# Second cross-attention: the score maxima subtracted as three bf16 pieces in one bf16 product

## The reference, cut to what matters

```
q, k, v = query @ wq + bq, key @ wk + bk, value @ wv + bv      # key = value = context, 77 tokens
score = einsum('bhqd,bhkd->bhqk', q, k) / sqrt(16)
score = score + (1 - mask) * -1e9
alpha = softmax(score, axis=-1)                                # subtracts the row's maximum
x = einsum('bhqk,bhkd->bhqd', alpha, v) @ wo + bo
```

## Time and profile before

| | us |
|---|---|
| median of 3 runs (lowest, highest) | 2876.49 (2875.19, 2884.41) |
| the profiled execution, its own time | 2881.71 |
| its span, first to last instruction | 2880.0 |
| outside the span | 1.7 |
| PE busy in the span | 2053.4 |
| DVE busy | 2194.8 |
| ACT busy | 1748.7 |
| mean granted TensorE clock | 0.753 |

### The profile page before, as it was taken

One profiled execution on the slowest core, in us unless ns is written; L12 is line 12 of the kernel. 1 busy time (PEld: TensorE's weight loads), 2 busy tenths in 40 slices (PEclk: granted clock), 3 DMA queues, 4 the chain that ended last, 5 costly groups with the idle time before them and its releaser, 6 DMA issues. The chain is left out here.

```text
span 2880.0 us, 41500 instructions
## 1 busy us (share of the span) xinstructions
PE 2053.4 (71%) x11052; PEld 1159.4 (40%) x11052; DVE 2194.8 (76%) x10063; ACT 1748.7 (61%) x5698; POOL 652.8 (23%) x343
## 2 busy tenths in 40 slices
PE   6232555646556465555657599999999999799997
PEld 3122434434334343343444333334343343465554
DVE  5999999999999999999997355555555555276677
ACT  3678888888888888888881244444444444222221
POOL 0000000000000000000000166766767667200000
PEclk9555556555565555655555699999999999799999
DMA  5742222222222222222210000000000000201100
GB/s 113 152 103 49 50 69 52 55 56 66 49 52 59 63 55 49 58 64 52 55 33 4 4 13 12 13 16 16 11 13 16 15 13 12 88 8 45 41 11 8
DMA packets 86798, 123.55 MB, mean 43 GB/s; under 512 B 17444, under 2 KB 65224, under 8 KB 86600
## 3 DMA queue, kind: packets, MB, share of 16 engines
q1 hardware_dynamic: 86600, 121.37, 17.7%
HBM read 100.33 MB, written 21.00 MB: 42 GB/s over the span
## 5 line engine op out<-in xcount | busy, mean ns | idle before, releaser
L1494 ACT ACTIVATE mix_cand<-mix_pre,mixer_cbuf 128x32 f32<-128x32 f32 x2048 | 591.3, 289 | 166.0 <-DVE mix_pre L1424 82.3
L1491 ACT ACTIVATE mix_cand<-mix_state,mixer_cbuf 128x32 f32<-128x32 f32 x2048 | 652.9, 319 | 34.9 <-DVE mix_state L1416 4.5
L1411 DVE SCALAR_TENSOR_TENSOR mix_prod<-mixer_keys,mixer_cbuf,mix_cand 128x65 f32<-128x65 f32 x2048 | 581.7, 284 | 34.3 <-ACT mix_cand L1494 27.2
L1925 DVE TENSOR_REDUCE self_tops<-self_rough 128x2 f32<-128x1024 f32 x256 | 313.5, 1225 | 365.8 <-PE self_rough L1697 362.6
L1424 DVE SCALAR_TENSOR_TENSOR mix_pre<-mixer_keys,mix_gap,mix_state 128x32 f32<-128x32 f32 x2048 | 526.1, 257 | 27.8
L1523 PE MATMUL mix_out<-all_ident,mix_state 128*128 128x128 f32 x512 | 161.9, 416 | 488.6 <-ACT mix_flat L1475 432.5
L1416 DVE SCALAR_TENSOR_TENSOR mix_state<-mix_cand,mixer_cbuf 128x32 f32<-128x32 f32 x2048 | 507.6, 248 | 0.1
L1911 POOL TENSOR_TENSOR self_psum<-self_psum,self_prob 128x1024 f32<-128x1024 f32 x192 | 451.5, 2352 | 128.3 <-ACT self_prob L1838 118.7
L1838 ACT ACTIVATE self_prob<-self_sco 128x1024 f32<-128x1024 f32 x256 | 260.4, 1024 | 117.1 <-PE self_sco L1710 102.4
L875 POOL TENSOR_TENSOR mix_st_norm_rstd<-mix_st_norm_var,mix_half 128x2 f32<-128x2 f32 x24 | 16.7, 697 | 1316.4 <-DVE mix_st_norm_var L868 1316.4
L1523 PEld LDWEIGHTS mix_out<-all_ident,mix_state 128*128 128x128 f32 x512 | 82.4, 206 | 571.2 <-ACT mix_flat L1475 504.8
(11 more groups left out here) (386 smaller groups left out, 3273.7 us busy)
## 6 DMA issues: line engine op xcount, KB each, us to landing
mixer_keys<-k_rows SPq DMA_DIRECT2D x256, 260.0 KB, 4.9
aT_rows<-self_aT SPq DMA_DIRECT2D x32, 256.0 KB, 2.3
two_aT<-aT_rows SPq DMA_DIRECT2D x8, 1024.0 KB, 7.3
coef_rows<-mixer_coef SPq DMA_DIRECT2D x4, 1280.0 KB, 7.3
mixer_cbuf<-coef_rows SPq DMA_DIRECT2D x64, 80.0 KB, 5.5
k_rows<-mixer_krow SPq DMA_DIRECT2D x32, 65.0 KB, 5.0
proj_xin<-in_xT SPq DMA_DIRECT2D x8, 256.0 KB, 3.3
mix_st_xin<-in_x SPq DMA_DIRECT2D x8, 256.0 KB, 5.5
```

What stands on the lines that cost most here:

```text
L1411: dve.scalar_tensor_tensor(prod[:, b, :], keys[:, h, b, s_, :], coef(NIB, h, s_, b), cand[:, b, s % 2, :], ALU.mult, ALU.mult, accum_out=g ...
L1491: act.activation(cand[:, b, (s + 1) % 2, NS:2 * NS], state[:, hp, sp_, b, :], ACT.Copy, scale=cbuf[:, h, KEEP, b, s_:s_ + 1]).then_inc(kep ...
L1494: act.activation(cand[:, b, (s + 1) % 2, 0:NS], pre[b], ACT.Tanh, scale=cbuf[:, h, BETA, b, s_:s_ + 1]).then_inc(c_ready[b], 1)
L1925: dve.tensor_reduce(tops[:, kh, t, :], rough[:, :, :], AX.X, ALU.max).then_inc(rough_taken, 1)
```

## The change

The maximum of each head is laid as three bf16 numbers whose sum is the f32 value: the first is the value rounded to bf16, the second the rest rounded, the third what is left. `pieces` holds them, `top_dve` makes them by five linked instructions (copy, subtract, copy, subtract, copy), and the two copies into `wide_top` carry 48 columns instead of 16: row 4i + n of a block of 32 holds piece i of head n. `topT` and `minus` become bf16, so the L739 product is a bf16 one over the same 32 rows. `minus` has -1 in the three rows of its head; its pattern comes from one more reduction in the setup (`nths`). The first layer keeps its f32 form.

```diff
-        self.minus = sb("minus", [P, 2 * KT, S2])
+        self.minus = sb("minus", [P, 2 * KT, S2], BF16 if keep_masked else F32)
+        self.ranks = 3 * 2 * KT if keep_masked else 2 * KT
...
-        yield dve.tensor_reduce(self.nth[:, :], self.ident[:, :].rearrange("p (c r) -> p r c", c=QUADS)[:, 0:2 * KT, :], AX.X, ALU.add)
+        yield dve.tensor_reduce(self.nth[:, :], self.ident[:, :].rearrange("p (c r) -> p r c", c=QUADS)[:, 0:self.ranks, :], AX.X, ALU.add)
+        if self.keep_masked:
+
+            yield dve.tensor_reduce(self.nths[:, :], self.nth[:, :].rearrange("p (i n) -> p n i", i=3), AX.X, ALU.add)
...
-        yield dve.tensor_scalar(self.minus[:, :, :], bcast(self.nth[:, :], 2, S2), -1.0, None, ALU.mult)
+        yield dve.tensor_scalar(self.minus[:, :, :], bcast(self.nths[:, :], 2, S2), -1.0, None, ALU.mult)
...
-        ... self.topT = ..., sb("topT", [P, GT])
+        ... self.topT = ..., sb("topT", [P, GT], BF16)
+        self.pieces = sb("pieces", [P, CTILES, 3, H], BF16)
...
-    LINKS = 1 + 1
+    LINKS = 1 + 5 + 1
...
         alone(link(ins))
+
+        for i in range(3):
+            alone(link(dve.tensor_copy(self.pieces[:, :, i, :], self.top[:, :, :])))
+            if i < 2:
+                alone(link(dve.tensor_tensor(self.top[:, :, :], self.top[:, :, :], self.pieces[:, :, i, :], ALU.subtract)))
         for j in range(CTILES):
-            ins = dve.tensor_copy(self.wide_top[:, j, :].rearrange("p (c r) -> p c r", c=QUADS)[:, :, 0:2 * KT].rearrange("p c (f e) -> p f c e", f=KT),
-                                  self.top[:, j, :].rearrange("p (f c e) -> p f c e", f=KT, c=QUADS))
+            ins = dve.tensor_copy(self.wide_top[:, j, :].rearrange("p (c r) -> p c r", c=QUADS)[:, :, 0:3 * 2 * KT].rearrange("p c (n e) -> p n c e", e=2),
+                                  self.pieces[:, j, :, :].rearrange("p i h -> p (i h)").rearrange("p (n c e) -> p n c e", c=QUADS, e=2))
```

More of the change, by code:

```diff
@@ L561, in setup_room @@
         self.piece = sb("piece", [P, B, S2], BF16)
-        self.nth, self.odd = sb("nth", [P, 2 * KT]), sb("odd", [P, 2])
+        self.nth, self.odd = sb("nth", [P, self.ranks]), sb("odd", [P, 2])
+        self.nths = sb("nths", [P, 2 * KT]) if self.keep_masked else self.nth
         self.loaded, self.kv_made, self.k_ready, self.set = sem("loaded"), sem("kv_made"), sem("k_ready"), sem("set")
@@ L641, in setups @@
     def setups(self):
-        return 2 + (not self.keep_masked) + 2 + 3 + 3 * 3 + KT * (1 + 3 * B)
+        return 2 + (not self.keep_masked) + 2 + 3 + self.keep_masked + 3 * 3 + KT * (1 + 3 * B)
 class CrossAttention:
@@ L653, in __init__ @@
         self.q, self.qb, self.prob = sb("q", [P, KT, GT]), sb("qb", [P, KT, GT], BF16), sb("prob", [S2, KT, QUADS, 2, GT])
-        self.top, self.wide_top, self.topT = sb("top", [P, CTILES, H]), sb("wide_top", [P, CTILES, P]), sb("topT", [P, GT])
+        self.top, self.wide_top, self.topT = sb("top", [P, CTILES, H]), sb("wide_top", [P, CTILES, P]), sb("topT", [P, GT], BF16)
+        self.pieces = sb("pieces", [P, CTILES, 3, H], BF16)
         self.rden, self.aT = sb("rden", [P, KT, GT]), sb("aT", [P, KT, GT])
```

## The result

The changed kernel takes 2889.2 us (median of 17 runs) against 2877.3 for the kernel before (17 runs). The ratio is 1.0035, 95% interval 1.0025 to 1.0045: slower by 7 to 13 us, some 10; the two medians lie 11.9 us apart. The profiled execution has a span of 2888.7 us against 2880.0, 8.7 more.

A forecast was written before the change was run, and what follows sets the result against it. PE was taken to bound e0 and the rough half, DVE both wide_top handovers, ACT the exponentials. Group shifts summed to +4.5 or +7.7 us; the middle, +6 on 2876.5, gave 2882.5 us, range 2875 to 2891.

The forecast's parts named there:

- The forecast's own band of +4 to +8: Whole kernel: the likeliest case, +4 to +8 us, 2880 to 2885 us, chance 0.60.
- the late clock: Values: rival that the clock returns late into them, 1.8 us a group over +7.7, +15, 2891 us; chance 0.20.
- The matmuls removed: L739 on PE: bf16 set of four 0.21 us at half clock, saving 0.64 or 0.32 a set, some 15 us PE time.
- The rival that the four do not run abreast: L739 on PE: bf16 products save nothing, DVE steps still paid, some +10, 2886 us; chance 0.04.
- The DVE steps: Handovers through wide_top: five linked instructions and wider copies add 1.2 us each (1.0 to 1.4), uncovered.
- The rival of cheap steps: Handovers through wide_top: added DVE work costs 0.7 us each, total +1.0, 2877.5 us; chance 0.09.
- Group by group: Start of the values, groups 0 to 3: shifts sum to +4.5 us with clock back before f1, +7.7 at the values.
- half-clock branch: f1 scores at 1.2 GHz until the values start: 0, +1.9, +2.9, +2.9 us for groups 0 to 3, sum +7.7.
- so I take the middle, +6: Clock's return around the f1 scores: +6 us chosen between +4.5 (back before f1) and +7.7 (back as values start).
- The prediction's own sign of being wrong: Attention pieces: wrong if the stretch at 0.50 differs by several microseconds, or two f0, not DVE, still releases ACT.
- The setup: Setup of minus: one more reduction (0.2 us) hides in DVE's 1.56 us idle gap, costs nothing; end unchanged.

The follow-up runs named there:

- The runs with 0 to 10 steps: Changed kernel with 0, 3, 5 (as changed) or 10 DVE steps in each handover; ratios to the kernel before 0.9976, 0.9999, 1.0035, 1.0051.
- the f32-product run: Changed kernel with topT and minus in f32 again, the five DVE steps and three pieces kept; ratio 1.0031 to the kernel before.
- the bf16 turn: Changed kernel with wide_top in bf16 and the turn as a bf16 product with a bf16 identity; ratio 1.0013 to the kernel before.
- split in one: Changed kernel with the five DVE steps in chain one only, chain two's maxima rounded straight to bf16; ratio 1.0007 to the kernel before.
- one piece: Kernel before with topT and minus in bf16, maxima rounded, no DVE step added; ratio 0.9976; traced twice, 2878.6 and 2880.5 us.
- ten steps: Changed kernel with five more linked casts to a spare tile in each handover; ratio 1.0051 to the kernel before.
- two pieces: Changed kernel with the third piece left out, three linked DVE steps instead of five; ratio 0.9999 to the kernel before.
- the second pair of traces: Kernel before and changed kernel, nothing altered, each profiled once more: 2882.3 and 2891.3 us.
- The run with PE kept busy: Changed kernel with useless f32 products ahead of the turn in PE's waits, three in chain one, two in chain two; ratio 1.0041 to the kernel before.

## Why the prediction was partly right

**The time and the verdict.** The forecast was 2882.5 us, +6, no change at 0.70; measured is +10, just beyond the 8.6 us that I had set as the bound, and 2889.2 us lies inside the range of 2875 to 2891. By that bound the kernel is slower, which had 0.25, though the interval of 7 to 13 us reaches below it. The forecast's own band of +4 to +8 was missed; the range holds because the late clock had been let into it. The mechanism held: two uncovered handovers against shorter sets, a small net loss. The sign and the size of most terms held too; one choice was off.

**The matmuls removed: right.** 0.21 us a set of four at half clock, as priced; a (f, e) set takes 1.28 us at half clock (in f32 1.93), which was priced at 1.29. The rival that the four do not run abreast is out.

**The DVE steps: right.** Priced at 1.2 us a handover; the first stretch grew by 1.13 (7.00 to 8.13), five times 0.22 and 0.03 for the wider copies, where I had put 0.08. The 0.3 us of cover in group 0 was there too. The runs with 0 to 10 steps show the 0.22 as a slope in both handovers. The rival of cheap steps is out.

**Group by group: right in its half-clock branch.** From first maximum to first values row: groups 1 to 3 take 26.28 us each, against 24.40, 23.37 and 23.37: +1.88, +2.91, +2.91, where the branch with the low clock lasting until the values had +1.9, +2.9, +2.9. Group 0 came at -0.67 (23.25 against 23.92), where I had -0.4 to 0. The sum is +7.0 against +7.7.

**The failed step: "so I take the middle, +6".** The trace of before left open when the clock would return, and I split the difference between +4.5 and +7.7, though both reasons named there, longer waits and shorter sets, spoke for the late end. It returned neither in the middle nor at the values' start but 1.3 us into them (values from 2623.98, clock at 2625.3 in group 1). That is the rival "the clock returns late into the values" in a mild form: from the first values row to the reciprocal 4.37, 4.27 and 4.21 us against 3.73, 1.7 us in all, where the rival had 1.8 a group. 7.0 + 1.7 is the 8.7 us of the pieces; the 10.1 +/- 3 of the ratio agrees with it. The prediction's own sign of being wrong says the same: it names a stretch at 0.50 that differs by several microseconds, and against the 13.6, 10.2 and 10.2 us of before they are 20.5. With it the start of the values, 17.0 us behind L744 of one, lies just outside the 15.9 to 16.9 that were named.

**What I had not seen.** That with the shorter product the clock returns later: the f32-product run has the same steps, low stretches of 13.7, 17.1 and 17.1 us against 20.5, and loses only 1.0 us on the changed kernel. The prediction counted the saving and the clock as two separate terms. They are coupled, here through where the second turn stands in the low stretch. That the product alone moves the clock is read from this one pair; shifts of 0.3 us (the bf16 turn) also took the stretch from 20.5 to 17.1 us in two groups of three, so where it ends answers to small shifts of any kind. The third stretch against the time from the second turn to the clock's return, in groups 1 to 3, over the traces with the f32 turn:

| kernel, group | clock back behind the second turn, us | third stretch, us |
|---|---|---|
| before, 1 | 5.2 | 13.20 |
| split in one, 2 | 8.0 | 13.18 |
| one piece, 1 | 9.2 | 13.26 |
| split in one, 1 | 9.8 | 13.52 |
| ten steps, 3 | 10.1 | 13.65 |
| changed, 1 | 11.1 | 14.17 |

The groups that are not in the table lie on the same line, two pieces in group 2 with 11.0 and 14.1 among them. Up to some 9 us the low clock costs nothing there, as far as these traces go: ACT's table and its three sets of exponentials (1.28 and 6.0 us) stand on the same way and set a floor of 13.2. Beyond it each microsecond costs about half of one. The changed kernel stands furthest out. With the bf16 turn the clock is back 8.3 and 9.8 us behind the second turn in groups 1 and 2, and only in group 3 still 10.7, which is why 0.29 us a turn gave 3.7.

**The setup: right.** The second layer does not start later (its first matmul of L2244 at 2479.66 us; L2233 of the kernel before at 2481.12).

**Open.** The cause that puts the first maximum of group 0 2.35 us earlier in the changed kernel (2.0 in the second pair of traces) was not tested by itself; part of it may be a shorter low stretch over the queries (3.4 against 6.8 us). The one-piece kernel shows both stretches, 3.4 and 6.8 us, in its two executions, with starts 3.1 us apart, so no change of the kernel is needed for it. Three to 4 us between medians and pieces in the one-piece and two-piece kernels are not explained either; the tails, which differ from one execution to the next by 2 us, may be part of it.

The Trainium skill (TensorE: Matmul & The Clock Gate, section "What's actually happening") says that activity releases the throttle. The run with PE kept busy does not bear that out as a remedy: filled waits kept the clock up through the second stretch of group 1 (6.43 us), and then it stood at 0.50 for 27.3 us with PE busy for 27.28 of them.

## What to carry to other kernels

Count what a change adds to a handover on the way between two engines before counting what it saves in the products behind it: here 1.13 us of small instructions bought 0.64 us of matmul, and the same bf16 product without the split (a shift that numerators and sum share need not be exact) is 0.24% faster than the kernel before. Where the granted clock moves, a saving is not a number but a function of where the low stretch ends; read that distance first, and give both ends when the trace does not fix it. Before a difference of 2 us in two traces is put down to a change, repeat each trace once.

## What the runs showed of the hardware

- A linked cast f32 to bf16 and a linked f32 subtraction, both of 128x32, take 0.18 and 0.19 us and follow each other by 0.22 us; the cast to bf16 is not cheaper in any way that counts.
- Four bf16 products of 32 rows by 256 columns in four row blocks advance the queue by 0.21 us at 1.2 GHz, the same as four of 3 rows; in f32 it was 0.85.
- The turn of two 128x128 tiles takes 0.69 us in f32 and 0.40 in bf16 at 1.2 GHz, and 0.44 and 0.28 at 2.4 GHz: far less than the factor four of the products of 256 columns.
- The stretches of the kernel before repeat from one execution to the next to within 0.1 us (109.98 and 109.99 us in all), and yet the one-piece kernel had tails of 68.5 and 66.5 us. The Trainium skill (TensorE: Matmul & The Clock Gate, section "What's actually happening") says that the number of slow matmuls changes from run to run; this pair of tails agrees.
- Work of no use in PE's waits moved the low stretch; in two of three groups it came back longer (27.3 and 37.5 us against 20.5), in one shorter (3.4 us).
